# Cross attention on one core: p's second high part behind two bank copies, and a last batch finished in other pieces

## The reference

```python
x_q = einsum('oc,bcn->bno', w_qk, y);  x_k = einsum('oc,bcn->bon', w_qk, x)
x_v = einsum('oc,bcn->bon', w_v, x) + b_v[None, :, None]
attention = softmax(einsum('bnc,bcm->bnm', x_q, x_k), axis=-1)
attention = attention / (1e-07 + attention.sum(axis=1, keepdims=True))
x_r = einsum('bcn,bnm->bcm', x_v, attention)
out = x + relu(einsum('oc,bcn->bon', w_t, x - x_r) + b_t[None, :, None])
```

## Time and profile before

| | |
|---|---|
| median of 3 runs | 1848.62 us (1848.58 to 1848.97) |
| the profiled execution | 1846.96 us, its span 1845.1 us |
| PE busy | 1839.9 us, 100% of the span, 8895 matmuls |
| DVE busy | 1500.8 us, 81% |
| ACT busy | 1309.9 us, 71% |
| POOL busy | 786.7 us, 43% |
| chain that ended last | PE 98%, ACT 1% |

### The profile page before, as it was taken

One profiled execution on the slowest core, in us unless ns is written; L12 is line 12 of the kernel. 1 busy time (PEld: TensorE's weight loads), 2 busy tenths in 40 slices (PEclk: granted clock), 3 DMA queues, 4 the chain that ended last, 5 costly groups with the idle time before them and its releaser, 6 DMA issues.

```text
span 1845.1 us, 26425 instructions
## 1 busy us (share of the span) xinstructions
PE 1839.9 (100%) x8895; PEld 1551.9 (84%) x8895; DVE 1500.8 (81%) x2034; ACT 1309.9 (71%) x1798; POOL 786.7 (43%) x421
## 2 busy tenths in 40 slices
PE   9999999999999999999999999999999999999999
PEld 8888888888888888888888888888888888888887
DVE  7878787787787877888878788788787877878878
ACT  7767766677666776667776677766677766776665
POOL 6543344442444424444244453344433444334431
PEclk9999999999999999999999999999999999999999
DMA  3101111011110111111122111111011110111201
GB/s 109 69 24 64 52 68 68 23 68 46 68 68 24 67 46 68 68 37 54 46 68 68 54 37 46 68 68 66 25 52 62 68 68 23 67 47 69 69 1 46
DMA packets 34090, 101.92 MB, mean 55 GB/s; under 512 B 4224, under 2 KB 5248, under 8 KB 34048
## 3 DMA queue, kind: packets, MB, share of 16 engines
q1 hardware_dynamic: 33760, 101.07, 15.8%
q10 hardware_dynamic: 288, 0.39, 0.1%
HBM read 67.90 MB, written 33.55 MB: 55 GB/s over the span
## 4 chain that ended last, share of the span: by engine, by line
PE 98%; ACT 1%; DMA 0%; DVE 0%; POOL 0%; issue 0%; SPq 0%; DVEq 0%; POOLq 0%; ACTq 0%
PE pv L781 37%; PE row_b L676 19%; PE row_a L676 14%; PE pv L753 9%; PE row_b L739 5%; PE row_a L739 5%; PE row_a L730 5%; PE row_b L730 5%; DMA y_raw<-y 0%; ACT y_hi L284 0%; ACT p_sb L323 0%; DVE colsum L519 0%; POOL gx_lo L223 0%; PE pv L869 0%; ACT z_hi L309 0%
## 5 line engine op out<-in xcount | busy, mean ns | idle before, releaser
L213 POOL TENSOR_TENSOR y_lo<-y_raw,y_hi 128x896 fp32r<-128x896 f32 (+1 forms) x128 | 277.3, 2191 | 545.9 <-ACT y_hi L284 356.3
L526 DVE SCALAR_TENSOR_TENSOR p_lo<-p_sb,row_inv,p_hi 128x1024 fp32r<-128x1024 f32 x254 | 325.4, 1282 | 96.0 <-ACT p_hi L331 95.9
L314 ACT ACTIVATE ev<-row_b 128x512 f32<-128x512 f32 x384 | 229.2, 597 | 199.1 <-PE row_b L676 198.9
L198 POOL TENSOR_TENSOR x_lo<-x_sb,x_hi 128x1024 fp32r<-128x1024 f32 x63 | 152.1, 2415 | 449.2 <-ACT x_hi L272 449.2
L323 ACT ACTIVATE p_sb<-p_sb,neg_max 128x1024 f32<-128x1024 f32 x256 | 295.1, 1154 | 28.9 <-DVE neg_max L501 24.9
L331 ACT ACTIVATE p_hi<-p_sb,row_inv 128x1024 fp32r<-128x1024 f32 x256 | 292.5, 1143 | 30.8 <-PE pv L781 30.0
L519 DVE SCALAR_TENSOR_TENSOR colsum<-p_sb,row_inv,colsum 128x1024 f32<-128x1024 f32 x224 | 292.5, 1306 | 8.5 <-DVE row_inv L509 0.6
L781 PE MATMUL pv<-p_hi,z_hi 128*128 128x512 f32 x1024 | 273.7, 389 | 0.0
L781 PE MATMUL pv<-p_hi,z_lo 128*128 128x512 f32 x1024 | 273.7, 389 | 0.0
L501 DVE CUSTOM_DVE_ANT_0 p_sb<-row_a,ev 128x1024 f32<-128x1024 f32 x128 | 156.6, 1223 | 142.7 <-PE row_a L676 142.7
L781 PE MATMUL pv<-p_lo,z_hi 128*128 128x512 f32 (+1 forms) x1047 | 271.7, 383 | 0.0
(11 more groups left out here) (142 smaller groups left out, 3580.5 us busy)
## 6 DMA issues: line engine op xcount, KB each, us to landing
x_sb<-x SPq DMA_DIRECT2D x64, 512.0 KB, 4.6
out<-res SPq DMA_DIRECT2D x62, 512.0 KB, 3.1
y_raw<-y SPq DMA_DIRECT2D x64, 256.0 KB, 3.6
y_raw<-y SPq DMA_DIRECT2D x32, 512.0 KB, 3.7
out<-res SPq DMA_DIRECT2D x2, 256.0 KB, 2.2
res<-w_qk SPq DMA_DIRECT2D x1, 256.0 KB, 2.9
res<-w_t_T SPq DMA_DIRECT2D x1, 256.0 KB, 6.9
res<-w_v SPq DMA_DIRECT2D x1, 256.0 KB, 7.5
```

The source lines that it names most:

```text
L213: nc.gpsimd.tensor_tensor(y_lo[:, of:, cols], y_raw[:, 1 + of:8, cols], y_hi[:, of:, cols].bitcast(FP32), ALU.subtract).then_inc(y_lo_done, 1)
L314: nc.scalar.activation(ev[:, to, :], bank_b, ACT.Copy, scale=scale).then_inc(b_copied, 1)
L526: nc.vector.scalar_tensor_tensor(out=p_lo[r][:, :], in0=p_sb[r][:, :], scalar=row_inv[:, j:j + 1], in1=p_hi[r][:, :].bitcast(FP32), op0=AL ...
```

## The change

ACT's `pair`: for t = 2 and 3, copy_e and the second copy_b now come ahead of p_high(t-1, 1), as they did for t = 1. In the last batch the third quarter of W x is done in two column halves, each with its own matmuls and its own signal, the second half in bank a. The scale of the fourth quarter moves from DVE to ACT (adds the constant) and GpSimd (multiplies). The second quarter's relu and addition of x, before on ACT and DVE, become one `finish_part` on DVE, for which ACT adds the bias to the right columns of x in pair 0 (`x_bias_last`).

```diff
@@ ACT: pair @@
-                elif t == 1:
+                else:
                     copy_e(b, t)
                     copy_b(b, t, 1, EV_U2, -1.0)
-                    if first:
+                    if t == 1 and first:
                         p_high(b, 0, 0, first)
                     p_high(b, t - 1, 1, first)
-                else:
-                    p_high(b, t - 1, 1, first)
-                    copy_e(b, t)
-                    copy_b(b, t, 1, EV_U2, -1.0)
...
+                if t == 0 and last:
+                    x_bias_last()
@@ pieces of the last batch @@
+        last_parts = ((0, left, pv[:, 0, left]), (0, right, pv[:, 0, right]),
+                      (1, slice(0, C), pv[:, 1, 0:C]), (1, slice(C, BANK), bank_a[:, 0:C]))
@@ GpSimd, behind the last two p_low @@
+            pool.wait_ge(apart_raised, 1)
+            nc.gpsimd.tensor_tensor(colsum[:, left], colsum[:, left], turn_buf[:, right],
+                                    ALU.mult).then_inc(apart_scaled, 1)
@@ ACT, behind the last batch @@
+            def x_bias_last():
+                act.wait_ge(x_lo_done, KT * (B - 1) + 1)
+                nc.scalar.activation(x_sb[1][:, 0, right], x_sb[1][:, 0, right], ACT.Identity,
+                                     bias=bias[:, 0:1]).then_inc(x_biased, 1)
...
-            for h in range(NH):
-                cols = slice(h * BANK, (h + 1) * BANK)
-                act.wait_ge(w_done, KT * (B - 1) + h + 1)
-                nc.scalar.activation(res[:, 0, cols], pv[:, 0, cols], ACT.Relu, bias=bias[:, 0:1]).then_inc(last_bent, 1)
+            act.wait_ge(last_pv, 2)
+            act.wait_ge(s_spread, B)
+            nc.scalar.activation(colsum[:, left], pv[:, 1, right], ACT.Identity,
+                                 bias=eps_wb[:, 1:2]).then_inc(apart_raised, 1)
+            act.wait_ge(w_done, KT * (B - 1) + 1)
+            nc.scalar.activation(res[:, 0, left], pv[:, 0, left], ACT.Relu, bias=bias[:, 0:1]).then_inc(last_bent, 1)
@@ DVE, behind the last batch @@
-            for q in range(KT * NH):
-                scale_quarter(B - 1, q)
+            for mt, cols, to in last_parts:
+                scale_part(B - 1, mt, cols, to)
             add_apart(B - 1)
             dve.wait_ge(apart_added, 1)
-            finish_part(B - 1, bank_c, right, last_out[3])
-            dve.wait_ge(last_bent, 2)
-            nc.vector.tensor_tensor(res[:, 0, right], res[:, 0, right], x_sb[1][:, 0, right],
-                                    ALU.add).then_inc(last_out[1], 1)
-            dve.wait_ge(w_done, KT * (B - 1) + 3)
+            finish_part(B - 1, 1, bank_c, right, last_out[3])
+            dve.wait_ge(w_done, KT * (B - 1) + 2)
+            finish_part(B - 1, 0, pv[:, 0, right], right, last_out[1])
             for h in range(NH):
-                cols = slice(h * C, (h + 1) * C)
-                finish_part(B - 1, pv[:, 1, cols], cols, last_out[2])
+                mt, cols, src = last_parts[NH + h]
+                dve.wait_ge(w_done, KT * (B - 1) + 3 + h)
+                finish_part(B - 1, mt, src, cols, last_out[2])
@@ PE, behind the last batch @@
-            for q in range(3):
-                pe.wait_ge(scaled, KT * (B - 1) + q + 1)
-                w_block(1, q // NH, q % NH).then_inc(w_done, 1)
+            for i, (mt, cols, dst) in enumerate(last_parts):
+                pe.wait_ge(scaled, KT * (B - 1) + max(i + 1, 4 * (i // NH)))
+                for kt in range(KT):
+                    for n, (w, v) in enumerate(((wtT_hi, x_hi), (wtT_lo, x_hi), (wtT_hi, x_lo))):
+                        last = nc.tensor.matmul(dst, w[:, kt, rows_of(mt)], v[1][:, kt, cols], start=False,
+                                                stop=(kt == KT - 1 and n == 2), skip_group_check=True)
+                last.then_inc(w_done, 1)
```

More of the change, by code:

```diff
@@ L132, in xattn_kernel @@
         w_apart, apart_added, last_bent = sem("w_apart"), sem("apart_added"), sem("last_bent")
+        apart_raised, apart_scaled = sem("apart_raised"), sem("apart_scaled")
         last_stored = sem("last_stored")
@@ L572, in finish, with scale_part, finish_part @@
                                                op1=ALU.add).then_inc(out_ready, 1)
-            def scale_quarter(b, q):
-                mt, cols = q // NH, slice(q % NH * BANK, (q % NH + 1) * BANK)
+            def scale_part(b, mt, cols, to):
                 dve.wait_ge(s_spread, b + 1)
                 dve.wait_ge(last_pv, mt + 1)
-                nc.vector.scalar_tensor_tensor(out=pv[:, mt, cols] if q < 3 else colsum[:, left], in0=pv[:, mt, cols],
-                                               scalar=eps_wb[:, mt:mt + 1], in1=turn_buf[:, cols], op0=ALU.add,
-                                               op1=ALU.mult).then_inc(scaled, 1)
+                nc.vector.scalar_tensor_tensor(out=to, in0=pv[:, mt, cols], scalar=eps_wb[:, mt:mt + 1],
+                                               in1=turn_buf[:, cols], op0=ALU.add, op1=ALU.mult).then_inc(scaled, 1)
             def add_apart(b):
                 dve.wait_ge(w_apart, 1)
-                dve.wait_ge(scaled, KT * b + 4)
+                dve.wait_ge(apart_scaled, 1)
                 nc.vector.tensor_tensor(bank_c, bank_c, colsum[:, left], ALU.add).then_inc(apart_added, 1)
[L588 to L592, removed]
+            def finish_part(b, mt, src, cols, done):
+                dve.wait_ge(x_biased, KT * b + mt + 1)
+                dve.wait_ge(out_stored[mt], DMA * b)
+                nc.vector.scalar_tensor_tensor(out=res[:, mt, cols], in0=src, scalar=neg_bias[:, mt:mt + 1],
+                                               in1=x_sb[b % 2][:, mt, cols], op0=ALU.max,
+                                               op1=ALU.add).then_inc(done, 1)
             def pair(b, t):
```

## The result

The changed kernel takes 1860.41 us (median of 4 runs, 1859.75 to 1860.79) against 1848.60; the ratio of the runs is 1.0064, with a 95% interval of 1.0052 to 1.0076. The forecast was 1861.0. The profiled execution took 1860.51 us, its span 1858.6, 13.5 more than before.

The account below looks back on a forecast made before the run. PE (TensorE) was taken to bound the kernel, with steady batches of 57.16 us of unbroken matmuls. 11.8 for 31 turns plus 0.6 for the end (1.02 - 0.44) made 12.4, so 1861.0 us on the median 1848.62; range 1857 to 1866.

Parts of the forecast that it names:

- The worked-out steps: Pair 3 on DVE, spaced as in pair 1: p_low 1.18 us behind p_high, the next p_low 6.54 behind that.
- Turn: DVE's entry into the end of each batch, forecast 0.69 us late because of pair 3's late p_high.
- DVE's gap of 0.23: DVE's wait for ACT just before z_low, forecast to swallow 0.23 of the 0.69 us delay, letting 0.46 through.
- The wait per turn: p1's weight load waiting for z_low at each batch's start: 0.38 us, 31 times, 11.8 us; bounds 0.30 and 0.46.
- this seam: Next batch's start, where p1 waits for z_low: 0.23 us of DVE gap and 0.07 of slack swallow 0.30.
- One sign: Ahead of p_low(2,1) in pair 3, DVE was to wait some 3.6 us for p_high.
- Pair 2 costs nothing: Later y_high in pair 2 pushes pair 3's copy_b, leaving 0.14 us before p6's load; costed at nothing.
- Rival 2: ACT late too: pair 3's copy_b over 0.14 us later than worked out makes p6 wait, 5.0 more, 1866.0; 8%.
- The last batch: PE's last low pass waits for GpSimd's two p_low, released by a later p_scaled: everything after 1.02 us later.
- The tail's term: Behind the last matmul, one 256-column finish instead of two taking 0.88: 0.44 us less, at most.
- The rule on the empty pipe: At z_low, next Vector operation starts only once the pipe is empty; strictly, wait 0.46, 14.3 us in all; not adopted.
- The sum, 12.4: Whole kernel: 11.8 us for 31 batch turns plus 0.6 for the end, giving 1861.0 us.

Follow-up runs that it names:

- z_first: The whole change, with DVE making z's first low part ahead of the second scale of pv; 1848.38 us against 1847.99 for the kernel before, ratio 1.0005.
- the doses: Two kernels: the change's new end with ACT's old order, plus one or two repeated DVE instructions between turn and z_low; 1849.03 and 1856.05 us against 1847.52.
- order_t3: The whole change, but with ACT's new order in pair 3 alone, pair 2 keeping the old one; 1859.49 us against 1847.99 for the kernel before, ratio 1.0066.
- dose2: The change's new end with ACT's old order, plus a repeated reduce and a repeated reciprocal on DVE per batch; 1856.05 us against 1847.52 for the kernel before.
- order_only: The kernel before with only ACT's order changed for t = 2 and 3, keeping its own end; 1860.46 us against 1847.99, ratio 1.0072.

## Why the prediction was right

**The chain held step by step.** The worked-out steps, p_low 1.18 behind p_high and 6.54 to the next, are in the trace after to the hundredth. Turn came 0.67 us later behind its batch's p1 load (1788.27 - 1744.03 against 1775.32 - 1731.75), where 0.69 was worked out. DVE's gap of 0.23 was used up as said: from turn to z_low it is 12.01 in place of 12.24. The wait per turn, 0.38 forecast, measured 0.39; with 31 turns 12.1 for 11.8. z_first shows that nothing but this seam carries it, the doses that it starts at 0.31 to 0.34 where 0.30 was worked out, order_t3 that it is pair 3.

**One sign was worked out wrongly.** DVE was to stand some 3.6 us ahead of p_low(2,1), its old 1.61 and the 2.04 of p_high; it stands 2.38. The sum left out that pair 2's reorder makes DVE's own work in front of it 1.27 later (3.65 - 1.27 = 2.38); in order_t3, where pair 2 keeps the old order, the longest such wait is 3.7. It changes no term of the forecast, since p_high comes last there either way.

**Pair 2 costs nothing,** as costed: its y_high pushes the copy of bank b to 1775.78 to 1776.36, and p6's load at 1776.56 doesn't wait; 0.15 us were left after the 0.05 of handover, 0.14 forecast. Rival 2 is out.

**The last batch** lost 1.00 (1.02 forecast), through GpSimd's p_low as said.

**The tail's term was twice too large, and it stood on the wrong path.** 0.44 was to be won because one finish stands behind the last matmul instead of two; 0.22 came (9.83 to 9.85 in the ten traces with the new end, 10.06 in the two with the old). The last finish does end earlier behind the last low pass, 6.64 in place of 6.96, which is 0.32. Of the 0.12 that are missing to 0.44, 0.07 are PE's: from the first load of W to the last matmul's end it takes 4.46 instead of 4.39, as the last twelve matmuls, of 256 columns, follow one another by 0.12, more than half of the 0.227 of a 512-column step. 0.04 is the last finish, which takes its whole 0.48 when it stands alone, where I counted a step of 0.44.

But the span doesn't end with that finish. It ends 0.48 behind the landing of the last of five stores, before and after, and the stores keep the DMA engines full. Two us behind PE's last work, before and after, as in the earlier trace rows (us, busy time of PE, PEld, DVE, ACT and POOL, PEclk, DMA share, GB/s):

```profile
1841.60:1843.60 2.00, 0.00 (x0) 0.00 (x0) 0.45 (x2) 0.00 (x0) 0.00 (x0) 1.00 1.02 371
1855.30:1857.30 2.00, 0.00 (x0) 0.00 (x0) 0.13 (x1) 0.00 (x0) 0.00 (x0) 1.00 1.00 363
```

Counted from the last low pass, the five stores land at 7.23, 7.93, 8.63, 9.11 and 9.58 us before, and at 7.00, 7.69, 8.41, 8.89 and 9.36 after: each is 0.22 to 0.24 earlier, as the first of them is issued 0.23 earlier (4.96 in place of 5.19). That first one is the fourth quarter. Its addition on DVE stood here in the kernel before:

```profile
1838.76 0.70 DVE L586 TENSOR_TENSOR row_b<-row_b,colsum 128x512 f32<-128x512 f32 x1
```

It starts 3.45 behind the last low pass now (1852.24 - 1848.79), 3.67 before (1838.76 - 1835.09). So the 0.22 came from the scale that moved to ACT and GpSimd, which the prediction costed at nothing. dose2 fits this: its last finish ends at 6.82, 0.18 later than in the change, and its last store still lands at 9.35. This is read from the traces; no run tried the pieces of the end one by one.

**The rule on the empty pipe** (the Trainium skill, "VectorE: DVE Perf Modes", section "The DRAIN you can't avoid"). Its strict form would have made the wait 0.46; the step of 2.39 behind two scales busy for 2.48, and 0.39 of wait, speak against the strict form here. The same section adds that a next operation that is not held starts earlier, and gives no amount.

The sum, 12.4, came out at 11.8 between medians and 13.5 between the two spans; executions of the changed kernel differ by 1 us, those of the kernel before on other chips by 2. The terms as the traces measure them add up to 31 x 0.39 + 1.00 - 0.22 = 12.9. They lie 0.5 above the forecast's 12.4 and the medians 0.6 below it, so that the median comes so close is partly luck; the scatter is as large.

## What to carry to other kernels

Where one engine is saturated and another runs its queue in order, ask of each moved instruction what it now waits behind, and follow the delay through the queues to the first place where the saturated engine reads the result: there a gap here and some slack there swallow a fixed amount, and only the rest counts, times the loop. An existing stage with the order that is planned elsewhere (here pair 1) gives the new spacings almost exactly. Before moving work on the producer's side, look whether the consumer's queue can take the critical item first: one swapped line undid 12 us. And look at what really ends the span: here the last stores keep the DMA engines full, so what counted was how early the first of them started, not how short the last computation was.

## What the runs showed that was not expected

The kernel with no slack passes on what the others hide. In one batch DVE stands still for 0.38 us between a reciprocal and the column sum:

```profile
518.28 1.28 DVE L532 SCALAR_TENSOR_TENSOR colsum<-p_sb,row_inv,colsum 128x1024 f32<-128x1024 f32 x1 [0.38 <-DVE row_inv L522]
535.15 0.19 PEld L687 LDWEIGHTS row_b<-gx_hi,y_hi 128*128 128x128 f32 x1 [0.64 <-DVE z_lo L499]
```

and p1 waits 0.36 longer than in the other batches (turn comes 44.64 behind its batch's p1 load, 44.29 in most). The traces of order_only and order_t3 have the same 0.64 in the same batch, and the kernel before has two such idle times of the column sum, without any wait on PE (its waits: total, times, longest):

```profile
DVE colsum L519 <- DVE row_inv L509: 0.6, 2, 0.4
```

In that batch of the kernel before, DVE's idle for ACT ahead of p_low(3,1) is 0.17 in place of 0.51, and turn is not late. z_first has the 0.38 and the late turn too (44.59), and no wait on PE. What halts DVE there stays open.
